# Six-layer decoder on one core: weights of the last three layers fetched and prepared inside the layer ahead, output stored batch by batch

## The chip, the cores and the metric

One core of one Trainium2 chip runs the whole program. The time is that of the device in microseconds (us), median of the runs. The engines are TensorE (PE), VectorE (DVE), ScalarE (ACT), GpSimd (POOL) and SyncE (SP, which only issues DMAs here); each runs its own instructions in order and waits for the others by semaphores.

## What is computed

Eight batches of x (256 x 512, float32) pass through six layers. After each, x becomes the layer norm of x plus the layer's output. In order:

```python
# attn0:  16 heads of 128, causal, rotary positions, one shared k/v head with gates
# xattn0: 32 heads of 16, keys and values from ctx_1024, axial rotary positions
# ffn0:   gated ffn of 1408, 8 experts of low rank on top of it, 2 chosen per token
# attn1:  16 heads of 32 over 4 kv groups, causal
# xattn1: 16 heads of 128 over 8 kv heads, keys and values from ctx_1024
# ffn1:   act_quant(rmsnorm(x)) @ ternary(w).T, hidden 2048, w3(silu(w1) * w2)
def _ternary_quant(w):
    s = jnp.mean(jnp.abs(w))
    wq = jnp.round(jnp.tanh(w / (s + EPS))) * jnp.arctanh(s)
```

A ternary weight is thus the sign of w where |w| is above a threshold that comes from the mean of |w| over the whole matrix, and zero elsewhere; the factor arctanh(s) is applied later (`c127`). All other weights and activations enter TensorE as a pair of float16 numbers, high and low part, and each product is three matmuls (high x high, high x low, low x high; `three`, L99).

## The kernel before

`build` (L2371) holds x in SBUF for the whole program and calls the six layers one after the other. Each layer is a `Scope`: it takes SBUF and semaphores, runs some blocks, and at its end POOL clears its semaphores in a block of its own (L70). A block ends when all engines have come to its end, so nothing of the next layer begins before. All loops over batches and heads are unrolled; within a layer's main block each engine has its own list, and the pipeline between them is written out by hand.

- **Weights.** Each of the first five layers begins with `load_and_split` (L106): SP issues 512 KB pieces (128 x 1024 float32) into a ring of 14 stages, ScalarE casts a piece to float16 (L137), VectorE subtracts the result from the piece and writes the low part (L143). TensorE and POOL have nothing to do in this block.
- **Counters.** In attn0, ffn0 and xattn1 the semaphores that count per batch start from one; a block of SP increments sets them (L90).
- **x.** In these three layers SP copies each batch of x within SBUF into `xcur` (L160), and TensorE transposes from there (L151); ScalarE and VectorE split the transposed x (L173, L180). A ninth, empty batch is copied and transposed at the end.
- **attn1** is `small_attention` (L707): steps t, one head each, with the projections, transposes and norms of neighbouring batches put into steps by a table (`at`). Per step ScalarE does the exponential and a cast, VectorE a maximum, POOL the low part of the probabilities.
- **xattn1** (L1604 and after): per batch 16 projections through four PSUM banks, then for i in 0 to 18: scores of head i, transposes of i-2, product with v of i-3, output projection of i-5. VectorE's list in one i is maximum, reciprocal of i-1, low part of the probabilities of i-2 and of the output of i-3; ScalarE's is the cast of i-2, the exponentials of i, the cast of i-3.
- **ffn1** (L1978) begins with `ternary_weights` (L1909): three 4 MB loads, Sign and Abs over 8192 columns per matrix on ScalarE, the sum of |w| on VectorE, one matmul that adds over partitions, then one compare-and-multiply per matrix (L1972). The gains g1, g2, g3 are fetched at the start of the main block (L2035), and POOL waits for them. The main block runs over 16 tiles of 128 rows, with four tiles in flight; iteration t of each engine's list works on tiles t to t-4.
- **Output.** After ffn1's scope has ended, one DMA of 4 MB stores all of x (L2432).

## Time and profile before

| what | us |
|---|---|
| median of 3 runs (lowest, highest) | 3574.78 (3571.34, 3575.84) |
| the profiled execution | 3574.41, its span 3572.6 |
| TensorE busy | 2898.9 (81%) |
| VectorE busy | 2107.8 (59%) |
| ScalarE busy | 1787.9 (50%) |
| POOL busy | 1404.3 (39%) |

Busy shares are means over stages with different limits, so they are read by stage. The page's forty slices (89 us each) show where TensorE dips, and where DMA is busy at the same time:

```profile
PE   3899989884888883899999778865999999952786
PEclk9988898996999996999999989987999999985998
DMA  4000000001000003000000000003000000030001
```

In a timeline row the columns are start, duration, engine, line, operation, tile written <- tiles read, shapes, count, and in brackets the idle time of the engine before it with the instruction that ended it. SPq rows are DMA issues.

### The profile page before, as it was taken

Reading aid. Unit: us, or ns where it says so; the run is one execution under the profiler, and the core shown is the slowest. Engines: PE = TensorE matmul, PEld = TensorE weight load, DVE = VectorE, ACT = ScalarE, POOL = GpSimd, SP = SyncE. Lnnn points to the kernel's source line nnn. Section 1 sums busy time; section 2 is a strip of 40 time slices with the busy share of each in tenths; the row PEclk is TensorE's granted clock in tenths of the full one; section 3 lists DMA queues with packets and bytes.
Section 4 is the critical chain, followed back from the end, with each engine's and each line's share of the span. In section 5 each row is a group of like instructions: output and inputs, shape, how many; then the busy total and the mean of one; then the engine's idle time right before and its main releaser. Section 6 shows DMA issues by size and latency. Waiting matters only on the chain. (4 is left out here: it accounts for less than half of the span.)

```text
span 3572.6 us, 64599 instructions
## 1 busy us (share of the span) xinstructions
PE 2898.9 (81%) x24890; PEld 2048.9 (57%) x24890; DVE 2107.8 (59%) x4526; ACT 1787.9 (50%) x3852; POOL 1404.3 (39%) x1539
## 2 busy tenths in 40 slices
PE   3899989884888883899999778865999999952786
PEld 2566655552566662777777666654666676631332
DVE  4666666665677775454455455655555555556886
ACT  3444444443788885233222256644444444445775
POOL 1333333332788883345444424440121112112553
PEclk9988898996999996999999989987999999985998
DMA  4000000001000003000000000003000000030001
GB/s 166 7 7 7 7 7 1 7 7 63 1 2 2 2 2 131 20 7 7 7 7 13 25 10 2 2 24 131 7 7 7 7 7 7 7 138 22 1 1 48
DMA packets 35031, 83.08 MB, mean 23 GB/s; under 512 B 5283, under 2 KB 9381, under 8 KB 33574
## 3 DMA queue, kind: packets, MB, share of 16 engines
q1 hardware_dynamic: 34726, 78.95, 5.9%
q8 instruction: 199, 3.26, 0.4%
q14 instruction: 106, 0.87, 0.1%
HBM read 60.59 MB, written 4.19 MB: 18 GB/s over the span
## 5 line engine op out<-in xcount | busy, mean ns | idle before, releaser
L873 POOL TENSOR_TENSOR c_pT<-c_prob,c_pT 128x512 f16<-128x512 f32 x256 | 293.3, 1159 | 106.5 <-ACT c_pT L832 105.8
L1686 POOL TENSOR_TENSOR c_prob<-c_prob,c_inv 128x512 f32<-128x512 f32 x128 | 133.2, 1041 | 244.1 <-DVE c_inv L1880 244.1
L1064 ACT ACTIVATE c_prob<-psT 128x512 f32<-128x512 f32 x256 | 155.9, 609 | 69.9 <-PE psT L995 56.0
L873 POOL TENSOR_TENSOR a_pT<-a_prob,a_pT 128x384 f16<-128x384 f32 x128 | 117.8, 924 | 183.6 <-ACT a_pT L832 183.5
L1143 DVE TENSOR_REDUCE c_peak<-psS 128x2 f32<-128x512 f32 x256 | 170.0, 684 | 20.6 <-PE psS L976 17.2
L832 ACT CAST c_pT<-c_prob 128x512 f16<-128x512 f32 x256 | 159.6, 624 | 0.0
L345 POOL TENSOR_TENSOR a_q_rot<-a_q_cos,a_q_sin 128x512 f32<-128x512 f32 x64 | 81.1, 1267 | 196.3 <-DVE a_q_sin L590 196.3
L1820 ACT CAST c_pT<-psT 128x512 f16<-128x512 f32 x128 | 75.1, 586 | 153.2 <-PE psT L1698 153.2
L353 POOL TENSOR_TENSOR a_prob<-a_prob,a_inv 128x128 f32<-128x128 f32 x128 | 51.3, 401 | 254.6 <-DVE a_inv L622 254.6
L520 ACT ACTIVATE a_pT<-psT,a_kvh_t 128x256 f16<-128x256 f32 (+1 forms) x256 | 93.8, 418 | 104.1 <-PE psT L366 104.1
L1390 POOL TENSOR_TENSOR f_ch<-f_h,f_c 128x256 f32<-128x256 f32 x88 | 76.3, 867 | 147.3 <-DVE f_h L1581 147.3
L101 PE MATMUL psP<-a_wq,a_xT 128*128 128x512 f16 x320 | 121.4, 379 | 13.6 <-DVE junk L594 10.4
L228 POOL TENSOR_TENSOR ln_rstd<-ln_ve,minus_half 128x1 f32<-128x1 f32 x48 | 32.0, 666 | 251.3 <-DVE ln_ve L213 251.3
L1812 ACT ACTIVATE c_prob<-psS,c_negmax 128x256 f32<-128x256 f32 x256 | 119.6, 477 | 21.7 <-DVE c_negmax L1873 20.7
L628 DVE SCALAR_TENSOR_TENSOR a_pT<-psT,a_kvh_t,a_pT 128x256 f16<-128x256 f32 (+1 forms) x256 | 95.0, 413 | 59.0 <-ACT a_pT L520 58.4
L1586 DVE TENSOR_TENSOR f_chs<-f_ch,f_chs 128x768 f16<-128x768 f32 x88 | 107.4, 1221 | 33.0 <-ACT f_chs L1526 32.3
L1873 DVE TENSOR_REDUCE c_negmax<-psS 128x2 f32<-128x512 f32 x128 | 88.3, 690 | 65.3 <-PE psS L1744 65.3
L976 PE MATMUL psS<-c_kS,c_qS 128*128 128x256 f16 x512 | 104.2, 288 | 25.4 <-DVE c_peak L1143 22.8
L103 PE MATMUL psP<-a_wq,a_xT 128*128 128x512 f16 x320 | 121.3, 379 | 0.0
L102 PE MATMUL psP<-a_wq,a_xT 128*128 128x512 f16 x320 | 121.3, 379 | 0.0
L2068 POOL TENSOR_TENSOR f_hg<-f_h,f_g 128x512 f32<-128x512 f32 x64 | 81.5, 1273 | 99.2 <-DVE f_h L2269 99.2
L1679 POOL COPY c_seen_now<-c_seen_col 128x2 f32<-128x2 f32 x9 | 1.7, 186 | 300.1 <-DVE c_qT L1866 253.0
(565 smaller groups left out, 11483.1 us busy)
## 6 DMA issues: line engine op xcount, KB each, us to landing
f_stage<-in_f_up_gateT SPq DMA_DIRECT2D x16, 352.0 KB, 7.9
c_stage<-in_L_xattn_Wq SPq DMA_DIRECT2D x10, 512.0 KB, 6.7
a_xcur<-x_all SPq DMA_DIRECT2D x9, 512.0 KB, 2.9
f_xcur<-x_all SPq DMA_DIRECT2D x9, 512.0 KB, 2.9
c_xcur<-x_all SPq DMA_DIRECT2D x9, 512.0 KB, 2.9
x_all<-in_x SPq DMA_DIRECT2D x1, 4096.0 KB, 13.9
a_stage<-in_L_attn_WqT SPq DMA_DIRECT2D x8, 512.0 KB, 7.5
a_stage<-in_L_attn_WoutT SPq DMA_DIRECT2D x8, 512.0 KB, 10.0
```

The source lines that it names most:

```text
L101: pe.matmul(out, a_hi, b_hi, start=first, stop=False, skip_group_check=True)
L102: pe.matmul(out, a_hi, b_lo, start=False, stop=False, skip_group_check=True)
L103: return pe.matmul(out, a_lo, b_hi, start=False, stop=last, skip_group_check=True)
L628: last = dve.scalar_tensor_tensor(pT[1][:, r, m, m * P:N], T[:, m * N + m * P:(m + 1) * N], kvh_t[:, m, H + h:H + h + 1], pT[0][:, r, m, m ...
L832: copy(pT[0][:, c % NPH, :], prob[:, c % NPX, :]).then_inc(p_high(c)[0], 1)
L873: pool.tensor_tensor(pT[1][:, c % NPH, :], prob[:, c % NPX, :], pT[0][:, c % NPH, :], ALU.subtract)\
L976: last = pe.matmul(S[:, first:first + w], qS[:, b % 2, h // HB, n * P:(n + 1) * P], kS[:, b % 2, k_of(h), 0:w], start=True, stop=not causa ...
L1064: act.activation(prob[:, c % NPX, :], ST[c % 2][:, 0:EW], ACT.Exp).then_inc(s.e_done, 1)
L1143: dve.tensor_reduce(peak[:, h, :], S, X_AXIS, ALU.max).then_inc(s.m_done, 1)
L1586: dve.tensor_tensor(chs[1][:, t % 2, :, :], ch[:, t % 2, :, :], chs[0][:, t % 2, :, :], ALU.subtract).then_inc(s.ch_lo.handle, 1)
L1686: pool.tensor_tensor(prob[:, h % NPB, :, :], prob[:, h % NPB, :, :], inv[:, h % NPB, :].rearrange("p (n a) -> p n a", a=1).broadcast_to([P ...
L1812: last = act.activation(prob[:, r, n, :], S[:, n * N:(n + 1) * N], ACT.Exp, bias=negmax[:, r, n:n + 1], accum_out=sums[:, r, n:n + 1])
```

## The change

1. Counters start from zero; the block that set them is gone. A wait for zero is left out (`after`). SBUF is laid out by hand (`place`, `plan`), so that weights of a later layer can be written while an earlier one runs.
2. TensorE transposes x straight from its place; the copies to `xcur` and the ninth batch are gone.
3. A class `Feed` fetches pieces of 512 KB into a ring of 3 or 4 stages (SP), and has calls for ScalarE and VectorE that handle one piece each, put into the lists by hand:
   - ffn0: 5 pieces (Wq, Wkv, Wo of attn1), one at the end of each of batches 1 to 5.
   - attn1: 16 pieces (Wk, Wv, context, Wq of xattn1), one every sixth step.
   - xattn1: 8 pieces of its own Wo in the projections of batch 0; 24 sums of |w| over 1024 columns of ffn1's matrices in batches 1 to 4 (every second head, on VectorE); the mean and threshold at the start of batch 7; 16 ternary pieces of w1 and w2 in batch 7, one per head. The gains are fetched in batch 7.
   - ffn1: 8 ternary pieces of w3 in iterations 1 to 3; the first output matmul waits for all of them.
4. Ternary pieces come in two kinds by turns: "sign" (Sign and Abs on ScalarE, one VectorE instruction) and "signs" (two VectorE instructions).
5. `load_and_split` is no longer called in attn1 and xattn1, and `ternary_weights` is gone.
6. The output is stored per batch from ffn1's main block.

```diff
+class Feed:
+    def fetch(self, sp, n):
+        for i in range(self.fetched, self.fetched + n):
+            if i >= self.ring:
+                sp.wait_ge(self.done, i - self.ring + 1)
+            sp.dma_start(self.staged(i), self.items[i][1]).then_inc(self.landed[i % self.ring], 16)
...
+    def high(self, act, n):
+        for i in range(self.high_at, self.high_at + n):
+            kind, src, hi, lo = self.items[i]
+            if kind == "split":
+                self.has_landed(act, i)
+                act.copy(hi, self.staged(i)).then_inc(self.high_done, 1)
+            elif kind == "sign":
+                self.has_landed(act, i)
+                act.activation(hi, self.staged(i), ACT.Sign).then_inc(self.signed, 1)
+                self.signs += 1
+                act.wait_ge(self.signed, self.signs)
+                act.activation(self.staged(i), self.staged(i), ACT.Abs).then_inc(self.high_done, 1)
...
+    def low(self, dve, n):
+        for i in range(self.low_at, self.low_at + n):
+            kind, src, hi, lo = self.items[i]
+            raw = self.staged(i)
+            if kind == "sum":
+                self.has_landed(dve, i)
+                last = dve.tensor_reduce(lo, raw.rearrange("p k (a n) -> p (k a) n", n=256), X_AXIS, ALU.add,
+                                         apply_absolute_value=True)
+            elif kind == "split":
+                dve.wait_ge(self.high_done, self.highs[i])
+                last = dve.tensor_tensor(lo, raw, hi, ALU.subtract)
+            elif kind == "sign":
+                dve.wait_ge(self.high_done, self.highs[i])
+                last = dve.scalar_tensor_tensor(hi, raw, self.thr[:, lo:lo + 1], hi, ALU.is_gt, ALU.mult)
+            else:
+                self.has_landed(dve, i)
+                m = self.mask[:, self.masks % 2, :].rearrange("p (k n) -> p k n", k=raw.shape[1])
+                dve.tensor_scalar(m, raw, self.thr[:, 3 + lo:4 + lo], None, ALU.is_lt).then_inc(self.masked, 1)
+                self.masks += 1
+                dve.wait_ge(self.masked, self.masks)
+                last = dve.scalar_tensor_tensor(hi, raw, self.thr[:, lo:lo + 1], m, ALU.is_gt, ALU.subtract)
+            last.then_inc(self.done, 1)
...
 # turn_x
-    pe.wait_ge(*s.xcur_ready.count(b, 16))
-            last = pe.transpose(banks[n][:, k * P:(k + 1) * P], xcur[:, n, k * P:(k + 1) * P], G.ident[:, :])
+                last = pe.transpose(banks[n][:, k * P:(k + 1) * P], G.x[:, b * NT + n, k * P:(k + 1) * P], G.ident[:, :])
...
 # small_attention: at the end of a step, ScalarE's and VectorE's list
+        def feeds(t):
+            return feed is not None and t >= 0 and t % 6 == 3 and t // 6 < len(feed.items)
+                    if feeds(t):
+                        feed.high(act, 1)
+                    if feeds(t):
+                        feed.low(dve, 1)
...
 # ffn0: behind the last hidden tile of a batch, ahead of the split of the next x
+                    if 1 <= b <= len(feed.items):
+                        feed.high(act, 1)
+                    if 1 <= b <= len(feed.items):
+                        feed.low(dve, 1)
                     x_low(dve, b + 1, s, xT, G.psS)
...
 # xattn1, ScalarE
+                        if b == 0 and i % 2:
+                            feed.high(act, 1)
+                    if b == B - 1:
+                        act.wait_ge(w_step, 5)
+                        act.activation(logs[:, 0, :], s_mean[:, :], ACT.Ln, bias=1.0)
+                        act.activation(logs[:, 1, :], s_mean[:, :], ACT.Ln, bias=1.0, scale=-1.0).then_inc(logs_done, 1)
...
                         if i >= 3:
                             hi_o(i - 3)
+                        if b == B - 1:
+                            feed.high(act, SIGNS[i])
...
 # xattn1, VectorE
+                        if b == 0 and i % 2:
+                            feed.low(dve, 1)
...
                         if i >= 3:
                             lo_o(i - 3)
+                        if 1 <= b <= 4 and 4 <= i < 16 and i % 2:
+                            feed.low(dve, 1)
+                        if b == B - 1:
+                            feed.low(dve, SIGNS[i])
...
 # ffn1
+                feed.fetch(sp, len(fed))
+                for b in range(B):
+                    sp.wait_ge(s.x_done, NT * (b + 1))
+                    sp.dma_start(G.out[:, b * NT:(b + 1) * NT, :], G.x[:, b * NT:(b + 1) * NT, :]).then_inc(out_done, 16)
...
+                    if 1 <= t <= 3:
+                        feed.high(act, (0, 3, 3, 2)[t])
...
+                    if 1 <= t <= 3:
+                        feed.low(dve, (0, 3, 3, 2)[t])
```

## Rows read from the trace of the kernel before

**Rows 1.** Busy time by stretch: length, PE, PEld, DVE, ACT, POOL, clock, DMA, GB/s

```profile
2404.20:2443.20 39.00, 0.00 (x0) 0.00 (x0) 29.35 (x24) 25.12 (x24) 0.00 (x0) 0.50 0.85 323
3183.80:3261.40 77.60, 0.59 (x2) 0.50 (x2) 53.28 (x14) 44.27 (x11) 0.16 (x3) 0.50 0.47 182
2910.00:3000.00 90.00, 84.90 (x635) 62.63 (x634) 46.31 (x94) 39.23 (x113) 18.17 (x19) 1.00 0.02 7
2210.00:2250.00 40.00, 33.46 (x437) 25.57 (x436) 23.65 (x59) 24.78 (x53) 18.48 (x21) 1.00 0.01 1
3387.00:3404.00 17.00, 13.79 (x74) 6.48 (x73) 14.65 (x31) 12.40 (x19) 9.01 (x8) 0.90 0.00 1
```

**Rows 2.** Timeline, start of ffn0's main block

```profile
1427.24 0.18 DVE L143 TENSOR_TENSOR f_wr<-f_stage,f_wr 128x32 f16<-128x32 f32 x1
...
1434.74 1.97 PE L156 MATMUL psS<-ident,f_xcur 128*128 128x128 f32 x8 [50.32 <-DMA f_xcur<-x_all]
```

**Rows 3.** Timeline, load ahead of attn1

```profile
2046.96 0.92 SPq L131 DMA_DIRECT2D a_stage<-in_L_attn_Wq  x2
...
2050.91 1.05 ACT L137 CAST a_wq<-a_stage 128x1024 f16<-128x1024 f32 x1 [17.20 <-DMA a_stage<-in_L_attn_Wq]
...
2058.97 0.35 SPq L843 DMA_DIRECT2D a_bias<-in_L_attn_bo  x1
```

**Rows 4.** Timeline, load ahead of xattn1 and start of its main block

```profile
2404.23 4.27 SPq L131 DMA_DIRECT2D c_stage<-in_L_xattn_Wq  x8
...
2412.44 1.22 DVE L143 TENSOR_TENSOR c_wq<-c_stage,c_wq 128x1024 f16<-128x1024 f32 x1 [0.59 <-ACT c_wq L137]
...
2443.19 0.24 SPq L1669 DMA_DIRECT2D c_seen_row<-in_seen  x1
```

**Rows 5.** Timeline, ternary block and start of ffn1's main block

```profile
3183.79 0.39 SPq L1931 DMA_DIRECT2D f_raw<-in_L_ffn_w1T  x1
...
3196.24 7.03 ACT L1943 ACTIVATE f_wq<-f_raw 128x8192 f16<-128x8192 f32 x1 [23.57 <-DMA f_raw<-in_L_ffn_w1T]
...
3227.07 26.08 DVE L1972 SCALAR_TENSOR_TENSOR f_wq<-f_raw,f_thr,f_wq 128x8192 f16<-128x8192 f32 x3
...
3240.13 1.28 ACT L1948 ACT_TABLE_LOAD   x1
...
3261.37 2.34 POOL L2052 TENSOR_TENSOR f_xg<-x_all,f_g 128x1024 f32<-128x1024 f32 x1 [7.55 <-DMA f_g<-in_L_ffn_g]
```

**Rows 6.** Timeline, end of ffn1 and the output

```profile
3556.25 0.55 DVE L2322 TENSOR_SCALAR x_all<-ln_r,ln_mv,ln_rstd 128x512 f32<-128x512 f32 x1 [0.66 <-POOL ln_rstd L2079]
3559.80 0.40 SPq L2432 DMA_DIRECT2D out_dram<-x_all  x1
```

**Rows 7.** Timeline, one head of xattn1 in batch 7, and the next maximum

```profile
3160.09 0.69 DVE L1873 TENSOR_REDUCE c_negmax<-psS 128x2 f32<-128x512 f32 x1 [0.59 <-PE psS L1744]
...
3161.01 0.48 ACT L1812 ACTIVATE c_prob<-psS,c_negmax 128x256 f32<-128x256 f32 x1
...
3161.92 0.38 ACT L1825 CAST c_qT<-psO 128x256 f16<-128x256 f32 x1
...
3162.33 0.42 DVE L1889 TENSOR_TENSOR c_qT<-psO,c_qT 128x256 f16<-128x256 f32 x1 [0.49 <-ACT c_qT L1825]
...
3163.35 0.69 DVE L1873 TENSOR_REDUCE c_negmax<-psS 128x2 f32<-128x512 f32 x1 [0.59 <-PE psS L1744]
```

**Rows 8.** Timeline, tables of xattn0: TENSOR_SCALAR from SBUF to SBUF

```profile
851.88 0.23 DVE L682 TENSOR_SCALAR c_ang<-c_ang 128x128 f32<-128x128 f32 x1
852.14 0.29 DVE L684 TENSOR_SCALAR c_turns<-c_ang 128x256 f32<-128x256 f32 x1
```

**Rows 9.** Timeline, ffn1, first gate of the iteration behind t = 1

```profile
3293.59 0.75 DVE L2269 SCALAR_TENSOR_TENSOR f_h<-psS,f_ax,f_sil 128x512 f32<-128x512 f32 x1 [0.81 <-ACT f_sil L2187]
```

**Rows 10.** Timeline, ffn1, the last step of a norm beside POOL's product

```profile
3405.13 2.19 DVE L2322 TENSOR_SCALAR x_all<-ln_r,ln_mv,ln_rstd 128x512 f32<-128x512 f32 x1
```

**Rows 11.** Timeline, ffn1, the last output matmuls

```profile
3548.38 5.28 PE L2137 MATMUL psO<-f_wq,f_hq 128*128 128x512 f16 x16 [2.58 <-DVE ln_ve L2316]
```

More of the change, by code:

```diff
@@ L79, in sb @@
     def sb(self, name, shape, dt):
-        return self.stack.enter_context(self.nc.sbuf_tensor(f"{self.tag}_{name}", shape, dt))
+        here, self.at = self.at, self.at + span(shape, dt)
+        assert self.at <= self.end, (self.tag, name, self.at)
+        return place(self.nc, f"{self.tag}_{name}", shape, dt, here)
     def counter(self, name, per_seq):
-        self.counters.append(Counter(self.sem(name), per_seq))
-        return self.counters[-1]
+        return Counter(self.sem(name), per_seq)
     def sem(self, name):
@@ L88, in sem @@
         return self.sems[-1]
-    def start_counters(self):
-        with self.nc.Block() as block:
-            @block.sync
-            def _(sp):
-                for counter in self.counters:
-                    sp.sem_inc(counter.handle, 1)
 def three(pe, out, a_hi, a_lo, b_hi, b_lo, first, last):
@@ L120, in load_and_split @@
     hi_done, lo_done = sc.sem("w_hi"), sc.sem("w_lo")
-    with nc.sbuf_tensor(f"{sc.tag}_stage", [P, NSTAGE, G.STAGE], F32) as stage, nc.Block() as block:
+    stage = place(nc, f"{sc.tag}_stage", [P, NSTAGE, G.STAGE], F32, sc.at)
+    with nc.Block() as block:
         def staged(i, p, k, n):
@@ L146, in kt_view, with split_pieces @@
+def split_pieces(src, hi, lo, k, n):
+    K, M = src.shape[1], src.shape[2]
+    out = []
+    for c in range(0, M, n):
+        for k0 in range(0, K, k):
+            at = (slice(None), slice(k0, k0 + k), slice(c, c + n))
+            out.append(("split", src[at], hi[at], lo[at]))
+    return out
 def kt_view(w):
     return w.rearrange("(k p) n -> p k n", p=P)
-def turn_x(pe, b, s, G, xcur, banks):
-    pe.wait_ge(*s.xcur_ready.count(b, 16))
-    for n in range(NT):
-        for k in range(KE):
-            last = pe.transpose(banks[n][:, k * P:(k + 1) * P], xcur[:, n, k * P:(k + 1) * P], G.ident[:, :])
-        last.then_inc(s.x_turned.handle, 1)
@@ L173, in x_high @@
 def x_high(act, b, s, xT, banks):
-    for n in range(NT):
-        act.wait_ge(*s.x_turned.count(b, n + 1))
+    for n in range(NT if b < B else 0):
+        after(act, s.x_turned, b, n + 1)
         act.copy(xT[0][:, :, n * P:(n + 1) * P], banks[n][:, :].rearrange("p (k t) -> p k t", k=KE))\
@@ L180, in x_low @@
 def x_low(dve, b, s, xT, banks):
-    for n in range(NT):
-        dve.wait_ge(*s.x_hi.count(b, n + 1))
+    for n in range(NT if b < B else 0):
+        after(dve, s.x_hi, b, n + 1)
         at = slice(n * P, (n + 1) * P)
@@ L1282, in ffn0 @@
     NU = 4
-    with Scope(nc, "f0") as sc:
+    with Scope(nc, "f0", G.low) as sc:
         def pair(name, shape):
@@ L1637, in xattn1 @@
         ones_b = sc.sb("ones_b", [P, P], BF16)
+        up = Scope(nc, "c1", G.a1_at)
+        prob = up.sb("prob", [P, NPB, NT, N], F32)
+        larger = sc.sb("larger", [P, 2, 1024], F16)
+        drams = [kt_view(W[f"L1_ffn_w{i}T"]) for i in (1, 2, 3)]
+        fed = split_pieces(kt_view(W["L1_xattn_Wo"]), wo[0], wo[1], 2, E)
+        for i, d in enumerate(drams):
+            for j in range(8):
+                k, c = divmod(j, 2) if i < 2 else (j, 0)
+                src = d[:, k:k + 1, c * 1024:(c + 1) * 1024] if i < 2 else d[:, 2 * j:2 * j + 2, :]
+                fed.append(("sum", src, None, part[:, i, 4 * j:4 * j + 4]))
+        for c in range(4):
+            for i in range(2):
+                for k in (0, 2):
+                    at = (slice(None), slice(k, k + 2), slice(c * E, (c + 1) * E))
+                    fed.append((("sign", "signs")[len(fed) % 2], drams[i][at], G.w12[i][at], i))
+        feed = Feed(sc, "feed", up.sb("feed", [P, 3, 1024], F32), fed, G.thr, larger)
+        NSUM = 24
+        SIGNS = [1] * H + [0] * 3
         NQ, NK, NV = H // 2, KVH // 2, NT * 2
@@ L1763, in project @@
                     def project(h):
-                        pe.wait_ge(*s.o_lo.count(b, h + 1))
+                        after(pe, s.o_lo, b, h + 1)
+                        if b == 0 and h % 2 == 0:
+                            pe.wait_ge(feed.done, h // 2 + 1)
                         for n in range(NT):
@@ L2133, in down @@
                             pe.wait_ge(s.var_ready, t)
+                        else:
+                            pe.wait_ge(feed.done, len(fed))
                         for k in range(KH):
```

530 lines of the change are left out of this document (273 added, 257 removed).

## The prediction

> **What bounds the kernel now.** I read four views, in this order: busy time and granted clock over chosen stretches, the timeline where one layer ends and the next begins, the timeline inside one steady step of each layer that is to take in new work, and the DMA issues. No engine is the bound of the whole span; each layer has its own, and between layers the kernel is serial. The reader is to see two stretches in which TensorE does nothing: before xattn1 it runs no matmul in 39.0 us while DMA is 85% busy and VectorE and ScalarE split weights, and ahead of ffn1 it is busy 0.6 of 77.6 us [rows 1]. Inside xattn1 it is the other way round: TensorE is busy 84.9 of 90 us at full clock, VectorE 46 and ScalarE 39. attn1 is milder (33.5 of 40 us, VectorE 24, ScalarE 25), and ffn1 is a chain over all engines (13.8, 14.7 and 12.4 of 17 us) [rows 1]. So the change takes work from places where everybody waits for it and puts it where somebody else is the bound. The question is how much of it shows there.
>
> **What goes.**
> 1. The copy of x ahead of the first transposes. In ffn0 VectorE is done with the weights at 1427.42 and TensorE begins at 1434.74 [rows 2]. In between lie the block that starts the counters and one DMA of x; both go. A plain block boundary takes about 0.3 us, so 7.0 us. attn0 begins in the same way: another 7.0. The later copies ran a batch ahead and cost nothing, so nothing more is gained by them. The transposes for a ninth batch go too, at the ends of three layers; I leave them out (0 to 2 us).
> 2. The load and split ahead of attn1: from the first issue at 2046.96 to the main block at 2058.97 is 12.0 us [rows 3].
> 3. The same ahead of xattn1: 2404.23 to 2443.19, 39.0 us [rows 4]. The mask set-up behind it stays.
> 4. The ternary block ahead of ffn1 and the gains' DMAs behind it: POOL's first product starts at 3261.37; after the change it can start where the first weight DMA is issued now, 3183.79, plus 0.3 [rows 5]: 77.3 us.
> 5. The output. Now the last x is ready at 3556.80, clearing the semaphores takes until 3559.80, and the 4 MB store ends with the span at 3572.6 [rows 6]. After it only the last batch's 512 KB is open at 3556.80. A 512 KB load takes 3.95 us from issue to the cast that waits for it [rows 3]; I take that, then the same 3.0 us of clearing: end at about 3563.9, 8.7 us less.
> Sum of 1 to 5: 14.0 + 12.0 + 39.0 + 77.3 + 8.7 = 151.0 us.
>
> **What comes in.** A split piece of 1024 columns is a cast of 1.05 us on ScalarE [rows 3] and a subtraction of 1.22 us on VectorE [rows 4], which waits for the cast.
> - ffn0, 5 pieces, one at the end of batches 1 to 5, ahead of the split of the next x. Nothing hides all of it, and all of it showing is 5 x 1.22 = 6.1 us. The cast falls where ScalarE waits for TensorE; I take 0.5 a piece: 2.5 us (0 to 6.1).
> - attn1, 16 pieces, every sixth step of about 2.5 us. There is room on average (ScalarE is idle 15 of 40 us), but VectorE stops at the piece until ScalarE, a little behind in its own program, has cast it. Behind that wait stand the next maximum and the splits that free TensorE's banks. All showing: 16 x 1.22 = 19.5 us; none: 0. I take a third, 7 us. In ScalarE's and SP's queues nothing is late: the pieces are 16 us apart, a load takes 4.
> - xattn1, batch 0, 8 pieces of Wo in the projections: per two projections VectorE has 2 x 0.69 + 1.22, TensorE about the same. 0.5 us (0 to 4).
> - xattn1, batches 1 to 4, 24 sums of 1024 columns on VectorE, every second head. One head takes 3.26 us, and VectorE idles 0.59 at its end waiting for TensorE [rows 7]. A sum is taken as long as a subtraction of that size, 1.22: 0.6 too long, but the loop described below needs only 2.5 of the 3.26, so the next head takes it up. Only the sum at each batch's end shows: 2 us (0 to 24 x 0.6 = 14).
> - Small steps: two short chains on VectorE at the ends of batches 5 and 7, the means in batch 7, and two logarithms with the table loads around them (1.28 us each [rows 5]) at a place where ScalarE waits for scores: 3 us (1 to 6).
> - **xattn1, batch 7: 16 ternary pieces, one per head.** This is the large term. Half are "sign": Sign and Abs on ScalarE, then a compare-and-multiply on VectorE. Half are "signs": a compare and a compare-and-subtract, both on VectorE. Follow one head [rows 7]: maximum at 3160.09, first exponential can start 0.72 later, the cast of o starts 0.91 behind it (3161.01 to 3161.92), VectorE's subtraction 0.41 behind that, and it is free 0.47 later. That is a loop of 2.51 us through two in-order engines, and TensorE's 3.26 hides it. A piece is put at the end of this loop on both engines. Prices: Sign and Abs did 8192 columns in 7.03 us [rows 5], so 1024 are as the cast, 1.05 each, with the wait between them 2.13; the compare-and-multiply is 26.08 us for 3 x 8192, 1.06 ns a column, as the split: 1.23. The short compare is not in the trace at this size; a TENSOR_SCALAR takes 0.23 us for 128 and 0.29 for 256 columns [rows 8], which carried on gives 0.65 to 0.7 (up to 1.22 if it runs like a subtraction). Sign head: 0.72 + 0.91 + 0.37 (the cast of o) + 2.13 + 1.28 = 5.4 us. Signs head: 2.51 + 0.07 + 0.7 + 1.25 = 4.5. Eight of each: 79.2 us against 16 x 3.26 = 52.2. Cost 27 us. Lower end: only VectorE's work counts. It is busy half of a batch [rows 1], so less than 2 us a head, and a piece is 1.6 on average: 3.6 a head at most, 5 us in all. Upper end: the compare at 1.22: 31 us, more if TensorE's clock falls (below).
> - **ffn1, 8 ternary pieces of w3** in iterations 1 to 3 (3, 3, 2), ahead of the next iteration's first gate. ScalarE can begin Sign about when that gate starts now (3293.59 [rows 9]). Iteration 1 (sign, signs, sign): Sign and Abs 2.1, then 1.25 + 1.95 + 1.25 on VectorE: 6.6 later. Iterations 2 (signs, sign, signs) and 3 (sign, signs): 2.1 + 1.25 + 1.95 = 5.3 each. Of 17.2 us the iteration takes back 1 to 1.5 each time, since VectorE then doesn't wait for silu (0.81 [rows 9]): 14 us (8 to 22).
> Sum: 2.5 + 7 + 0.5 + 2 + 3 + 27 + 14 = 56 us.
>
> The profiled execution is 3574.4 us long (span 3572.6), as good as the median of 3574.8. 3574.4 - 151 + 56 = 3479.4, less 1 for the ninth transposes: **3478 us**, 2.7% faster.
>
> The engines' common port is a place where the trace speaks against moving work. VectorE's TENSOR_SCALAR of 512 columns takes 2.19 us where it runs beside POOL's product of 1024 columns, and 0.55 at the end, where POOL has none left [rows 6, 10]. In xattn1 POOL's product ends before the piece starts; in ffn1's second iteration it does not. The Trainium skill, "GPSIMD Engine Reference", section "Specifications", says that POOL's SBUF interfaces are shared with VectorE and contend with VectorE instructions in a two-port mode or with two SBUF inputs. By that rule the splits in attn1 would be stretched too, as both their inputs lie in SBUF, and the sum would be some 5 us higher; by the trace's row alone, only the compares are.
>
> **The rivals.**
> - The loop is looser than I think (12%). Speaks for it: VectorE and ScalarE are half idle in xattn1 [rows 1]. Then batch 7 costs 5 us instead of 27: 3456.
> - TensorE's clock falls (15%). In batch 7 it works 3.1 us (94% of 3.26) out of about 5. After an idle of 2.58 us its next 16 matmuls of 512 columns take 5.28 us, where 16 x 512 columns at 2.4 GHz are 3.4 [rows 11], and ffn1 as a whole shows a granted clock of 0.90 where xattn1 has 1.00 [rows 1]. At 1.2 GHz a head's 3.1 us of TensorE are 6.2, 1.2 over my 5.0; over 16 heads that is 19 us, with 3 more in ffn1: 3500.
> - It does not do what it says in attn1 and ffn0 (10%): all 21 splits show because of VectorE's wait. 25.6 instead of 9.5: 3494.
> - ScalarE must load a table for Sign after Silu in ffn1 (5%). After Exp it did not (Sign at 3196.24 with none ahead) [rows 5]; after Silu no row shows it. Six loads of 1.28: 3486. The Trainium skill, "ScalarE: Activation LUTs", section "Table sets: the hidden batching unit", counts abs and identity among the functions in every set and does not list sign there; it leaves this open, and no row decides it.
> - Slower than before (2%): the clock stays at 1.2 GHz through whole batches of xattn1, because the gaps in VectorE's loop keep TensorE waiting. A batch has 84.9 us of matmuls in 90 [rows 1]; at half speed it takes some 170, 80 more. From 96 / 80 = 1.2 such batches on, the change loses; with batches 1 and 7 both slow the time would be 3638.
>
> **How the numbers follow.** 56% for the forecast, with its own range of 3462 to 3495. The range for all: downwards to just beyond the loose loop, 3450; upwards past the clock case to 3510, where also attn1's upper end and ffn1's lie. What is left out (both upper ends together with a fallen clock, or all terms at their lower ends) is under 2 in 10. About 0.2% (7 us) is what a measurement of this kernel can tell from no change. Faster by more than that: 0.97; within: 0.01; slower: 0.02.
>
> **What would show it.** In the profile after: TensorE's first matmul of ffn0 7 us nearer to the last split; no gap over 12 us between layers behind ffn0; attn1 no more than 8 us longer; batches 1 to 4 of xattn1 at 90 us each, batch 7 at 115 to 120, with VectorE's maxima 4.5 and 5.4 us apart in turn; granted clock there at 0.9 or above; first ffn1 iterations 4 to 6 us longer, with no ACT_TABLE_LOAD between Silu and Sign; end of the span 7 us after the last x. A batch 7 of 95 us, or maxima 3.5 us apart, would kill my loop; an attn1 longer by 15 us or more would kill the third that I took.

## The result and the profile after the change

The changed kernel takes 3480.69 us (median of 4 runs, 3479.75 to 3482.29) against 3574.49 us (3571.34 to 3575.84) beside it: a ratio of 0.9743, 95% interval 0.9729 to 0.9757. The prediction was 3478. The profiled execution took 3481.1 us, 93.3 less than that of before, with a span of 3479.1 us. So the total gives little away; the terms do. Each was measured from landmarks in the timelines: the first DMA of a stage's main block, and the rows in which VectorE writes a finished tile of x (two a batch; the first of the two unless the table says last).

| term | predicted | measured | from |
|---|---|---|---|
| attn0's start | -7.0 | -5.3 | first projection 54.65 -> 49.37 |
| ffn0's start | -7.0 | -6.9 | first finished x, after the shift ahead of the stage |
| load ahead of attn1 | -12.0 | -11.7 | last batch's first x in ffn0 to attn1's main block: 18.18 -> 6.45 |
| load ahead of xattn1 | -39.0 | -39.0 | the same, attn1 to xattn1: 43.42 -> 4.39 |
| ternary block, gains | -77.3 | -77.6 | last tile of x in xattn1 to POOL's first product: 81.63 -> 4.01 |
| output | -8.7 | -9.9 | last x to the end of the span: 16.35 -> 6.42 |
| ninth transposes | -1 | -1.0 | ffn0's last batch 74.75 -> 73.71 |
| ffn0, 5 splits | +2.5 | +1.4 | batches 74.75 -> 75.03 |
| attn1, 16 splits | +7 | +8.4 | main block to last x: 341.78 -> 350.22 |
| xattn1 batch 0, Wo | +0.5 | +1.6 | main block to first x: 99.72 -> 101.33 |
| 24 sums | +2 | +2.0 | batches 1 to 4: 90.84 -> 91.35 |
| batch 7, with small steps | +30 | +29.6 | 90.84 -> 120.42 |
| ffn1, 8 pieces of w3 | +14 | +15.0 | first product to last x: 294.88 -> 309.92 |
| sum | -96 | -93.4 | |

Busy time and granted clock of chosen stretches of the changed kernel (columns as in [rows 1]): a part of attn1, the heads of xattn1's last batch, and two stretches at the start of ffn1.

```profile
2210.00:2250.00 40.00, 31.85 (x423) 25.63 (x422) 25.54 (x61) 25.38 (x53) 17.31 (x20) 0.96 0.12 38
3070.00:3142.00 72.00, 47.41 (x308) 30.82 (x305) 47.56 (x77) 43.26 (x105) 14.97 (x14) 0.95 0.36 117
3160.00:3200.00 40.00, 16.72 (x64) 6.88 (x64) 17.46 (x28) 18.08 (x26) 13.17 (x11) 0.67 0.18 61
3200.00:3260.00 60.00, 38.31 (x182) 17.49 (x183) 47.26 (x88) 41.20 (x57) 27.08 (x23) 0.81 0.09 30
```

In the second row TensorE is busy 47 of 72 us, where it had 85 of 90 [rows 1]; its clock was granted at 0.95 all the same. In this batch no engine is busy all the time: they wait for each other in turn.

Timeline of the changed kernel at the starts of attn0, ffn0, xattn1 and ffn1 (start, duration, engine, line; in brackets the idle time ahead and what ended it):

```profile
44.45 1.94 PE L248 MATMUL psS<-ident,x_all 128*128 128x128 f32 x8 [44.45 <-PEq L136]
48.02 1.29 DVE L263 TENSOR_TENSOR a_xT<-psS,a_xT 128x512 f16<-128x512 f32 x2 [3.49 <-DMA a_rope_k<-in_rope_k]
49.37 0.39 PE L114 MATMUL psS<-a_wkv,a_xT 128*128 128x256 f16 x1 [2.97 <-DVE a_xT L263]
...
1421.85 0.19 DVE L157 TENSOR_TENSOR f_wr<-f_stage,f_wr 128x32 f16<-128x32 f32 x1
1422.36 1.94 PE L248 MATMUL psS<-ident,x_all 128*128 128x128 f32 x8 [43.35 <-PEq L136]
...
2385.56 0.55 DVE L1316 TENSOR_SCALAR x_all<-ln_r,ln_mv,ln_rstd 128x512 f32<-128x512 f32 x1 [0.44 <-POOL ln_rstd L983]
2388.97 0.26 SPq L1787 DMA_DIRECT2D c_seen_row<-in_seen  x1
...
3158.75 0.55 DVE L297 TENSOR_SCALAR x_all<-ln_r,ln_mv,ln_rstd 128x512 f32<-128x512 f32 x1 [0.44 <-POOL ln_rstd L306]
3162.76 2.34 POOL L2149 TENSOR_TENSOR f_xg<-x_all,f_g 128x1024 f32<-128x1024 f32 x1
```

In ffn0 TensorE begins 0.51 us behind the start of the last split instead of 7.50 [rows 2]: the full 7.0. In attn0 it begins 6.8 us sooner too, but the bracket in the second row tells where 1.7 of that went: VectorE waits for the DMA of the rope tables before it splits x. In the kernel before, that DMA was issued just ahead of the copy of x (at 46.76 and 47.32) and landed while TensorE waited for the copy. Ahead of xattn1 and ffn1 some 4 us stand where there were 43 and 82 [rows 4, 5].

Two heads of xattn1's last batch, VectorE and ScalarE, from one maximum over a sign piece and a signs piece to the third (the answer to [rows 7]):

```profile
3088.39 0.68 DVE L2030 TENSOR_REDUCE c_negmax<-psS 128x2 f32<-128x512 f32 x1
3090.27 1.07 ACT L196 ACTIVATE f_wq<-c_feed 128x1024 f16<-128x1024 f32 x1
3090.42 0.42 DVE L2046 TENSOR_TENSOR c_qT<-psO,c_qT 128x256 f16<-128x256 f32 x1 [0.69 <-ACT c_qT L1966]
3091.38 1.06 ACT L199 ACTIVATE c_feed<-c_feed 128x1024 f32<-128x1024 f32 x1
3092.47 1.28 DVE L215 SCALAR_TENSOR_TENSOR f_wq<-c_feed,thr,f_wq 128x1024 f16<-128x1024 f32 x1 [1.62 <-ACT c_feed L199]
3093.67 0.68 DVE L2030 TENSOR_REDUCE c_negmax<-psS 128x2 f32<-128x512 f32 x1
...
3096.04 0.74 DVE L219 TENSOR_SCALAR c_larger<-c_feed,thr 128x1024 f16<-128x1024 f32 x1
3096.82 1.28 DVE L222 SCALAR_TENSOR_TENSOR f_wq<-c_feed,thr,c_larger 128x1024 f16<-128x1024 f32 x1
3098.03 0.68 DVE L2030 TENSOR_REDUCE c_negmax<-psS 128x2 f32<-128x512 f32 x1
```

The maxima are 5.28 and 4.36 us apart (predicted 5.4 and 4.5), in turn from the fourth maximum to the end of the batch. VectorE no longer waits for TensorE ahead of a maximum; it waits 1.62 us for ScalarE's Abs, and the next head waits behind that.

The first w3 pieces of ffn1 on VectorE, and the gate behind them (it answers to [rows 9]):

```profile
3196.23 1.28 DVE L215 SCALAR_TENSOR_TENSOR f_wq<-f_feed,thr,f_wq 128x1024 f16<-128x1024 f32 x1 [3.19 <-ACT f_feed L199]
3197.43 0.75 DVE L219 TENSOR_SCALAR f_larger<-f_feed,thr 128x1024 f16<-128x1024 f32 x1
3198.21 1.28 DVE L222 SCALAR_TENSOR_TENSOR f_wq<-f_feed,thr,f_larger 128x1024 f16<-128x1024 f32 x1
3199.41 1.28 DVE L215 SCALAR_TENSOR_TENSOR f_wq<-f_feed,thr,f_wq 128x1024 f16<-128x1024 f32 x1
3200.61 0.75 DVE L2370 SCALAR_TENSOR_TENSOR f_h<-psS,f_ax,f_sil 128x512 f32<-128x512 f32 x1
```

Silu's table stays loaded: no ACT_TABLE_LOAD stands between Silu and Sign. From first gate to first gate the first four iterations take 21.7, 19.8, 19.8 and 17.8 us, where they took 15.9, 15.3, 15.6 and 16.4. In the second iteration one compare meets POOL's product of 1024 columns and takes 1.70 us instead of 0.75, as the prediction had read it from [rows 10].

The end, the last x and the last store (answers to [rows 6]); the span ends at 3479.1:

```profile
3472.68 0.55 DVE L2423 TENSOR_SCALAR x_all<-ln_r,ln_mv,ln_rstd 128x512 f32<-128x512 f32 x1 [0.66 <-POOL ln_rstd L2176]
3473.25 0.37 SPq L2136 DMA_DIRECT2D out_dram<-x_all  x1
```

### The profile page after: what moved, and what is told of

Read it like the earlier page. It is cut to its first block and busy times, and to the rows that moved or that the text cites. A ratio compares the mean times of both kernels' runs of the same rounds, so it can differ in the third digit from the quotient of the medians.

```text
span 3479.1 us, 64422 instructions
## 1 busy us (share of the span) xinstructions
PE 2910.5 (84%) x24866; PEld 2050.9 (59%) x24866; DVE 2108.0 (61%) x4574; ACT 1764.8 (51%) x3865; POOL 1404.9 (40%) x1537
## 3 DMA queue, kind: packets, MB, share of 16 engines
q8 instruction: 199, 3.26, 0.4%
## 5 line engine op out<-in xcount | busy, mean ns | idle before, releaser
L2211 PE MATMUL psS<-f_wq,f_xq 128*128 128x512 f16 x256 | 81.6, 477 | 56.1 <-DVE f_h L2370 49.7
L569 ACT CAST a_qT<-psT 128x512 f16<-128x512 f32 x64 | 36.7, 586 | 163.4 <-PE psT L442 163.4
```

Of the source, the lines that this page charges most:

```text
L2211: last = pe.matmul(U[2 * (j % 2) + i][:, :], xq[:, t % 2, i * KE + k, :], w12[i][:, k, c * E:(c + 1) * E], start=k == 0, stop=k == KE - 1)
```

## The experiments

All kernels start from the changed kernel. Stages that an edit doesn't touch are compared by their own lengths, because attn0 and xattn0 differ by some us from one execution to the next (last section).

**Loop or work in the last batch.** The first experiment only swaps an order:

```diff
                             hi_p(i - 2)
+                        if b == B - 1:
+                            feed.high(act, SIGNS[i])
                         if i < H:
                             expo(i)
                         if i >= 3:
                             hi_o(i - 3)
-                        if b == B - 1:
-                            feed.high(act, SIGNS[i])
```

> The changed kernel with one edit: in xattn1's last batch ScalarE does Sign and Abs of a piece ahead of the exponentials of that head, not at the end of the step. Same instructions, other order. Two theories on why a head takes 5.28 us (sign piece) or 4.36 us (signs piece) there. Loop theory (mine): VectorE's maximum, ScalarE's exponentials and cast, VectorE's subtraction and the piece follow each other, and VectorE waits 1.62 us for Abs; with the edit Sign and Abs fall where ScalarE waits 1.5 to 1.9 us for the maximum, so a sign head goes from 5.28 to about 4.0, a signs head stays at 4.36: 8 x 1.3 = 10 us less, about 3470. Work theory: what an engine has to do in a head sets its length, and the order doesn't matter: 3481, heads as before.

Measured: 3463.94 us, ratio 0.969 (0.9674 to 0.9706). The last batch went from 120.42 to 108.91 us, 11.5 less; the rest of the difference lies in attn0 and xattn0, where nothing was changed. A sign head takes 3.63 us, a signs head 4.36 as before. (One is 4.94.) The edited kernel's timeline, ScalarE and VectorE:

```profile
3079.16 1.06 ACT L196 ACTIVATE f_wq<-c_feed 128x1024 f16<-128x1024 f32 x1
3080.26 1.06 ACT L199 ACTIVATE c_feed<-c_feed 128x1024 f32<-128x1024 f32 x1
3080.42 0.68 DVE L2030 TENSOR_REDUCE c_negmax<-psS 128x2 f32<-128x512 f32 x1
3082.86 1.28 DVE L215 SCALAR_TENSOR_TENSOR f_wq<-c_feed,thr,f_wq 128x1024 f16<-128x1024 f32 x1
3084.05 0.69 DVE L2030 TENSOR_REDUCE c_negmax<-psS 128x2 f32<-128x512 f32 x1
```

Sign and Abs now run while ScalarE would wait for the maximum, and VectorE's piece has no wait ahead of it. The same instructions in another order are 1.65 us a sign head cheaper: the loop theory holds, the work theory doesn't.

The second takes ScalarE out:

```diff
-                    fed.append((("sign", "signs")[len(fed) % 2], drams[i][at], G.w12[i][at], i))
+                    fed.append(("signs", drams[i][at], G.w12[i][at], i))
```

> The changed kernel with all 16 pieces of the last batch of xattn1 made by VectorE alone (compare, then compare and subtract: 2.03 us of VectorE against 1.28 for a sign piece). Loop theory: every head takes the 4.36 us of a signs head, 8 x 0.92 = 7.4 us less, 3473. Work theory: VectorE, which has 3.9 us of work in a signs head, is the busiest engine of the pair of heads and gets 8 x 0.75 = 6 us more to do: 3487.

Measured: 3469.25 us, 0.9706 (0.9689 to 0.9722). From the fourth maximum on every head takes 4.35 or 4.36, and the batch 110.54, 9.9 less. VectorE, the busier of the two, had 6 us more to do, and the batch became shorter: what went was its wait for ScalarE. The work theory doesn't allow that. Batches 1 to 6 kept their lengths to 0.01 us in both runs.

**How far a head with extra work may lag.** Sums in six heads in a row (the second kernel has `1 <= b <= 2 and 4 <= i < 16` in the same place, twelve in a row):

```diff
-                        if 1 <= b <= 4 and 4 <= i < 16 and i % 2:
+                        if 1 <= b <= 4 and 7 <= i < 13:
                             feed.low(dve, 1)
```

> The changed kernel with the six sums of a batch (xattn1, batches 1 to 4) in six heads in a row, not in every second. Now the maxima are 3.71 and 2.81 us apart in turn and a batch is 0.51 us longer than before. Loop theory: a head with a sum needs 2.51 + 1.21 = 3.72 us, so six in a row push TensorE back by 6 x 0.46 less the first one that a buffer takes up: each batch 1.5 to 2.5 us longer, 3488. Work theory: VectorE has 1.9 + 1.2 = 3.1 us of work in such a head, under TensorE's 3.26: no change, 3481.

Measured: 3475.29 us, 0.9721 (0.9705 to 0.9738), and batches of 91.40 us against 91.35: no further cost, where I had expected 1.5 to 2.5 us each. Maxima of one batch, the last two with a sum ahead of them and the two behind:

```profile
2556.19 0.68 DVE L2030 TENSOR_REDUCE c_negmax<-psS 128x2 f32<-128x512 f32 x1
2559.69 0.68 DVE L2030 TENSOR_REDUCE c_negmax<-psS 128x2 f32<-128x512 f32 x1
2562.06 0.68 DVE L2030 TENSOR_REDUCE c_negmax<-psS 128x2 f32<-128x512 f32 x1
2565.12 0.69 DVE L2030 TENSOR_REDUCE c_negmax<-psS 128x2 f32<-128x512 f32 x1 [0.60 <-PE psS L1875]
```

Five of the six heads with a sum take 3.50 us, not my 3.72; the first takes 3.70, as a head with a sum does in the changed kernel (3.71, and 2.81 for the plain one behind it). Why a row of them is quicker isn't shown. Six of them lag by 1.65 us in all, and the next two heads, 2.37 and 3.06 apart, make up 1.1 of it. So the buffer is deeper than the one head that I had given it. Does it have an end?

> The changed kernel with the 24 sums in two batches of xattn1 (1 and 2), twelve heads in a row. The run with six in a row showed heads of 3.50 us, 1.65 us of lag at their end against TensorE's 3.26 a head, and no cost. Buffer theory: VectorE can lag TensorE by only some 1.5 to 2 us before TensorE waits; twelve in a row would lag 3.1, so these batches take 1 to 2 us more than the 91.4 with six, while batches 3 and 4 fall back to 90.84. Work theory: VectorE's 3.1 us of work stays under 3.26, no limit: 91.4.

Measured: 3478.93 us in one run. Batches 1 and 2 take 94.87 us, 3.5 more than with six sums; batches 3 and 4 are back at 90.83. From the fifth maximum to the last, all eleven intervals are 3.50 us: 38.5 against 34.8 in a plain batch, 3.7 more, and the batch is 4.04 longer than a plain one. Nothing is left to catch up in, so the whole lag shows. That there is a cost speaks against the work theory, but 3.5 us is more than the 1 to 2 of the buffer theory: a lag of a fixed 1.5 to 2 us isn't always forgiven. What the two runs fit is that the heads behind make up what they can before the batch ends.

**attn1: wait or work.**

```diff
-                    if feeds(t):
+                    if feeds(t - 1):
                         feed.low(dve, 1)
```

> The changed kernel with VectorE's subtraction of a piece in attn1 one step later than ScalarE's cast. attn1 is 8.4 us longer than before the change; VectorE waits for the cast in 10 of 16 places, 14.0 us in all, and the subtractions are 19.6 us of work. If VectorE's wait is what shows (my prediction's reason), the cost falls to 2 to 4 us and the time to about 3476. If it is the work itself (19.6 us more of VectorE and 17 of ScalarE in a stage where TensorE is busy 0.83), the stage keeps its length: 3481.

Measured: 3474.48 us, 0.9715 (0.9698 to 0.9731); attn1 takes 347.19 us, 3.0 less than after the change, 5.4 more than before it. So the wait isn't all of the cost (2 to 4 us would have been left), and the work isn't either (nothing would have changed). Where this stage was untouched, it took 350.2 to 351.4 us in eight profiled executions; with this edit 347.16 to 347.19 in three. VectorE's waits for the cast fell from 14.0 to 2.7 us. But the 16 subtractions, 19.6 us before this edit (1.21 to 1.23 each), now take 23.0 us. Two of them with the POOL product that they meet:

```profile
2112.23 1.22 DVE L212 TENSOR_TENSOR c_wv<-a_feed,c_wv 128x1024 f16<-128x1024 f32 x1
2112.29 1.92 POOL L960 TENSOR_TENSOR a_pT<-a_prob,a_pT 128x384 f16<-128x384 f32 x1 [3.16 <-ACT a_pT L917]
...
2137.11 0.91 POOL L960 TENSOR_TENSOR a_pT<-a_prob,a_pT 128x384 f16<-128x384 f32 x1 [1.63 <-ACT a_pT L917]
2137.17 1.93 DVE L212 TENSOR_TENSOR c_cT<-a_feed,c_cT 128x1024 f16<-128x1024 f32 x1
```

The first of the two takes its usual time, 1.22 or 0.91 us. The second takes its own time plus nearly all that the first has left: 0.71 of 0.85 us in the lower pair, 1.0 of 1.16 in the upper; other pairs of this run also come out 0.13 to 0.15 short of the whole. The two don't share, they queue. The Trainium skill, "SBUF — State Buffer", section "SBUF: two separate sides", says so: the port pair of VectorE and GpSimd is an exclusive lock, held by whoever starts first for the whole instruction, when VectorE's operation has two SBUF inputs. The trace agrees with that but for these 0.14 us.

In the changed kernel none of the 16 subtractions was stretched. The ten that waited began within 0.02 us of the end of POOL's product: the cast of `a_pT` that releases the product stands directly ahead of the piece's cast in ScalarE's list, and both end together. At the other six no product was under way. But POOL's products met subtractions there too, two of them less than 0.1 us behind the start of one:

```profile
2175.51 1.22 DVE L212 TENSOR_TENSOR c_cT<-a_feed,c_cT 128x1024 f16<-128x1024 f32 x1
2175.58 1.92 POOL L960 TENSOR_TENSOR a_pT<-a_prob,a_pT 128x384 f16<-128x384 f32 x1 [0.32 <-ACT a_pT L917]
```

What are the other 5.4 us? Two kernels, each without one half of the work:

```diff
-                last = dve.tensor_tensor(lo, raw, hi, ALU.subtract)
+                if self.tag == "a1":
+                    last = dve.memset(raw[:, 0:1, 0:1], 0.0)
+                else:
+                    last = dve.tensor_tensor(lo, raw, hi, ALU.subtract)
```

```diff
-            if kind == "split":
+            if kind == "split" and self.tag == "a1":
+                pass
+            elif kind == "split":
...
-                dve.wait_ge(self.high_done, self.highs[i])
+                if self.tag == "a1":
+                    self.has_landed(dve, i)
+                else:
+                    dve.wait_ge(self.high_done, self.highs[i])
```

> The changed kernel without VectorE's 16 subtractions in attn1 (a one-element memset stands in for each; the low halves of xattn1's weights are zeros, set ahead of the stage, so the output is not the reference's); ScalarE's casts stay. What is read is the length of attn1's main block: 341.8 us before the change, 350.2 after, 347.2 with the subtraction one step later. What do the remaining 5.4 us consist of? Theory A: VectorE's work, stretched where it runs beside POOL; then casts alone cost at most 2 us: 342 to 344. Theory B: ScalarE's casts hold up the exponentials and the banks that ScalarE frees; then casts alone already cost 4 us or more: 346 and up.

> The counterpart: without ScalarE's 16 casts in attn1 (the high halves are zeros, set ahead of the stage, so the output is not the reference's); VectorE's subtractions stay and wait for the piece's DMA alone. Theory A (VectorE's work): 345 to 347 us of main block. Theory B (ScalarE's casts): 342 to 344.

Measured, one run each (3476.82 and 3486.91 us): main block 344.86 us without the subtractions, 351.44 without the casts. The first kernel isn't quite "casts alone": its memset still waits for the cast, 9.4 us in six places. So casts and waits together cost 3.1 us; subtractions without casts or waits cost 9.7, where the changed kernel with all three costs 8.4 (8.4 to 9.6 in the eight executions), and the one with the subtraction a step later 5.4. VectorE's subtractions are the larger part (theory A), but neither theory gives these numbers, and the terms don't add up: taking casts and waits away from the changed kernel saved nothing that can be seen. In the kernel without casts the subtractions take 22.4 us instead of 19.6, since seven of them begin while POOL's product runs; how much of the 9.7 that makes isn't shown. Which of VectorE's steps the subtraction delays where it stands, these runs don't tell; that stays open.

**ffn1: the pieces in the waits of the first iterations.**

```diff
-        fed = [(("sign", "signs")[j % 2], w3_dram[:, 2 * j:2 * j + 2, :], w3[:, 2 * j:2 * j + 2, :], 2) for j in range(8)]
+        fed = [("signs", w3_dram[:, 2 * j:2 * j + 2, :], w3[:, 2 * j:2 * j + 2, :], 2) for j in range(8)]
...
+                    if t <= 3:
+                        feed.low(dve, 1)
                     move_x(t)
+                    if t == 0:
+                        feed.low(dve, 2)
                     gate(t - 1, 3)
...
-                    if 1 <= t <= 3:
-                        feed.low(dve, (0, 3, 3, 2)[t])
+                    if t in (1, 2):
+                        feed.low(dve, 1)
```

> The changed kernel with the eight w3 pieces of ffn1 all made by VectorE alone and put where it waits while the first iterations fill the pipeline: one ahead of each of the first four moves of x, two behind the first, one at the end of iterations 1 and 2. Before this edit these eight cost 15.0 us. Gap theory (mine): VectorE's work costs only where no wait takes it; it waits 3.9, 4.2, 2.1, 1.7 and 1.5 us at the places chosen, a piece is 2.03 us, and at most 4 us of the 15 stay: about 3470. Work theory: 8 x 2.03 = 16 us of VectorE in a chain over all engines show wherever they stand: 3481.

Measured: 3464.47 us, 0.9705 (0.969 to 0.9719). From the last x of xattn1 to the last of ffn1 it is 303.40 us instead of 313.93: 10.5 of the 15.0 are gone and 4.5 are left. The first piece, with the move of x behind it:

```profile
3163.28 0.75 DVE L219 TENSOR_SCALAR f_larger<-f_feed,thr 128x1024 f16<-128x1024 f32 x1
3164.06 1.28 DVE L222 SCALAR_TENSOR_TENSOR f_wq<-f_feed,thr,f_larger 128x1024 f16<-128x1024 f32 x1
3167.22 0.69 DVE L2358 TENSOR_SCALAR f_xq<-psT 128x1024 f16<-128x1024 f16 x1 [1.87 <-PE psT L2198]
```

VectorE still waits 1.87 us behind it, so the piece cost nothing. The gap theory holds, if not to the number (at most 4 us were to stay, 4.5 did). VectorE's pieces are 18.2 us of work here and 14.2 in the changed kernel, and the stage is 10 us shorter.

**The last batch: use the projections.**

```diff
-    G.w12 = [f1.sb(f"wq{i}", [P, KE, 2048], F16) for i in range(2)]
+    w2 = f1.sb("wq1", [P, KE, 2048], F16)
+    f1.at = G.c1_at + 2 * span([P, KE, 2048], F16)
+    G.w12 = [f1.sb("wq0", [P, KE, 2048], F16), w2]
...
-        SIGNS = [1] * H + [0] * 3
+        SIGNS = [0, 1] * 8 + [0] * 3
...
+                        if b == B - 1 and i >= NK + NV:
+                            feed.low(dve, 1)
```

> The changed kernel with all 16 pieces of xattn1's last batch made by VectorE alone; the eight of w1 go into the place of wk and wv, which are free sooner, and are made in the query projections, one each, and the eight of w2 in every second head. Now this batch costs 29.6 us more than a plain one, and 19.7 with one VectorE piece in every head. Loop theory, with the buffer that the run with six sums in a row showed: a head with a piece takes 4.36, the next 2.4 to 2.8, the pair 6.8 to 7.2 against 6.52, so the heads cost 1 to 5 us; a projection has 0.69 + 2.03 = 2.7 us of VectorE against 2.6 of TensorE, 1 to 3 us in all; small steps 2: the batch at 95 to 101 us, the time about 3457. Work theory: the same 16 pieces, the same 19.7 us: 3471.

Measured: 3457.26 us, 0.9682 (0.9668 to 0.9697); the batch takes 96.83 us, 6.0 more than a plain one. Of these 6.0, 0.8 lie ahead of the first maximum, and from the first maximum to the last it is 47.35 us against 42.42. Most of that, 3.6 us, falls on the first four intervals, which are quick in a plain batch (7.65 us in all); from the fifth maximum on the heads are 2.37 and 4.37 apart in turn, 6.74 a pair against 6.52. In the projections VectorE works without a pause, one projection every 2.62 us:

```profile
3060.13 0.69 DVE L2017 SCALAR_TENSOR_TENSOR c_qT<-psO,c_qT 128x512 f16<-128x512 f32 x1
3060.74 0.74 DVE L219 TENSOR_SCALAR c_larger<-c_feed,thr 128x1024 f16<-128x1024 f32 x1
3061.52 1.28 DVE L222 SCALAR_TENSOR_TENSOR f_wq<-c_feed,thr,c_larger 128x1024 f16<-128x1024 f32 x1
3062.75 0.69 DVE L2017 SCALAR_TENSOR_TENSOR c_qT<-psO,c_qT 128x512 f16<-128x512 f32 x1
```

The same 16 pieces cost 19.7 us with one in every head and 6.0 here. The place decides.

**The output in one store again.**

```diff
-                for b in range(B):
-                    sp.wait_ge(s.x_done, NT * (b + 1))
-                    sp.dma_start(G.out[:, b * NT:(b + 1) * NT, :], G.x[:, b * NT:(b + 1) * NT, :]).then_inc(out_done, 16)
+                sp.wait_ge(s.x_done, NT * B)
+                sp.dma_start(G.out[:, :, :], G.x[:, :, :]).then_inc(out_done, 16)
```

> The changed kernel with one part undone: the output in one store of 4 MB behind the last x, no longer batch by batch. The last x is ready at 3472.7 and the span ends 5.9 us behind it (its end was 15.8 us behind it before). If the store alone made that difference: span end 15 to 16 us behind the last x, the time 9 to 10 us longer, 3490. Rival: most of it was the clearing of the semaphores, which now runs at another place; then 4 us or less.

Measured: 3486.21 us (3482.42 to 3489.14), 0.9758 (0.9744 to 0.9773). The last x starts at 3471.25 and the span ends at 3487.4, 16.15 us later against 6.42: 9.7 us more, with nothing else changed, out of 9.9 gained. So the single large store makes nearly all of the difference, and the place of the clearing next to none. The medians differ by 5.5 us only, within what attn0 and xattn0 do from one execution to the next.

**All together.** One kernel with the later subtraction in attn1, the two edits of xattn1's last batch and of ffn1, and in attn0

```diff
                 dve.memset(g_cum[:, 0:1], 0.0)
-                dve.wait_ge(consts, 32)
                 x_low(dve, 0, s, xT, G.psS)
+                dve.wait_ge(consts, 32)
```

> All edits that the theories call good in one kernel: VectorE's subtractions in attn1 one step later, w1 in the query projections and w2 in every second head of xattn1's last batch, w3's pieces in the waits of ffn1's first iterations, and in attn0 VectorE splits the first x before it waits for the rope tables' DMAs. That last wait took the place of the x copy: TensorE's first matmul came 6.8 us sooner, the first projection only 5.3. Expected of it: first projection at 47.6 instead of 49.4. If the savings add up: 3481 - 3 (attn1) - 23 (last batch) - 11 (ffn1) - 1.7 = 3442. If a later stage gives one back (ffn1's first iterations against a colder TensorE, say), 3450 or more.

Measured: 3439.2 us (3436.83 to 3440.46), 0.9631 (0.9618 to 0.9644). Stage by stage: first projection at 47.74 instead of 49.37 (main block at 44.34 and 44.40); attn1 347.16; the last batch 98.27; ffn1 304.90. These are 1.6, 3.1, 22.2 and 9.0 us less, 36 in all, and xattn0, which nobody touched, was 5 us shorter in this execution. The savings nearly add up. What is missing lies in the last batch, 1.4 us more than alone, and in ffn1, 1.5. The second can't be told from chance: where ffn1 was untouched, it took 312.5 to 314.7 us from xattn1's last x, and the next kernel, with the same ffn1, took 303.7. The first comes with the clock, in this kernel's timeline and stretch:

```profile
3071.16 0.66 PE L1825 MATMUL psT<-ident,c_prob 128*128 128x128 f32 x4 [2.60 <-POOL c_prob L1813]
3072.69 0.63 PE L115 MATMUL psP<-c_wo,c_qT 128*128 128x512 f16 x1
...
3070.00:3076.00 6.00, 4.84 (x23) 2.84 (x24) 4.67 (x8) 3.00 (x11) 2.08 (x2) 0.72 0.26 87
```

TensorE had stood still for 2.60 us; then its matmuls of 512 columns took 0.63 us instead of 0.38 and the granted clock of these 6 us is 0.72, partly at 1.2 GHz. The kernel with the last batch's edit alone has the same idle at the same place, and there the clock stayed at 2.4 GHz:

```profile
3083.75 0.66 PE L1825 MATMUL psT<-ident,c_prob 128*128 128x128 f32 x4 [2.60 <-POOL c_prob L1813]
3085.11 0.38 PE L115 MATMUL psP<-c_wo,c_qT 128*128 128x512 f16 x1
...
3082.58:3088.58 6.00, 4.83 (x35) 3.59 (x36) 4.67 (x9) 3.59 (x12) 2.08 (x2) 1.00 0.27 87
```

So the idle alone doesn't bring the fall; what decides it, these runs don't show. It is the rival that I gave 15%, at a fifteenth of its price.

Last, the sums moved into the query projections of batches 1 to 3 as well:

```diff
-                        if 1 <= b <= 4 and 4 <= i < 16 and i % 2:
-                            feed.low(dve, 1)
...
-                        if b == B - 1 and i >= NK + NV:
+                        if (b == B - 1 or 1 <= b <= 3) and i >= NK + NV:
                             feed.low(dve, 1)
```

> The kernel with all good edits (3439) and one more: the 24 sums of xattn1 stand in the query projections of batches 1 to 3, eight each, not in the heads of batches 1 to 4. A query projection gives 2.6 us to VectorE, which has 0.69 of work there; a sum is 1.21. Room theory: batches 1 to 4 fall from 91.35 to 90.84, 2.0 us less, 3437. Rival: a sum holds up the split that frees a bank, and each of the 24 shows with some tenths: 3440 to 3445.

Measured: 3438.44 us (3432.03 to 3442.27), 0.9628 (0.9615 to 0.9641). Batches 1 to 4 take 90.83 us each, as before any change, and xattn1's main block is 2.1 us shorter than in the kernel above. The total can't tell the two apart; the trace can. This is the fastest of all, 1.2% below the changed kernel by the medians.

## Why the prediction was right, and where it wasn't

**The gains** came out at 151.4 us against 152. Five of the seven are within 0.3 us, since each was a serial stretch that could be read off between two rows. Two were off, in opposite ways. In attn0 the step "so 7.0 us ... another 7.0" failed: I priced the start by its likeness to ffn0 and didn't ask what is late next. The DMA of the rope tables was, 1.7 us, and moving one wait behind the splits gave 1.6 back. The output gained 1.2 more than I took: the last 512 KB and the clearing took 5.9 us behind the last x, not 7 (and my own terms end at 3563.8, not 3563.9).

**The last batch** was right in mechanism: heads of 4.36 and 5.28 us against 4.5 and 5.4, and the two swaps show why. That its total came to 29.6 against 30 is partly luck. Of the 29.6, 29.1 lie between the first maximum and the last (71.48 us against 42.42), where I had put 27; 0.5 lie behind, and nothing ahead. I had taken every plain head as 3.26 us, but the first four intervals of a plain batch take only 7.65 us together, so the heads cost more than I said. The 3 us for small steps made up for it: the logarithms with their table loads end at 3071.42, 0.4 us behind the end of the first maximum, and don't show otherwise. With 29.6 us the loose loop (3456) falls. What I had not seen is how little of the price was needed: 11.5 of the 29.6 us went with the order of ScalarE's list alone.

**The sums** had the right price, 2.0, for the right reason: a head with a sum takes 3.71 us, the next 2.81, a pair 6.52 as without sums, and only the last one of a batch shows. That a single head is all that can make up a lag, as I then took it, doesn't hold: behind six sums in a row two heads did, behind twelve none was left.

**attn1** cost 8.4 against 7, within its bounds, and past the 8 that I had named as the most. "I take a third" was a guess, and that it came near is luck. I had named VectorE's wait for the cast as the cause. Casts and waits together cost 3.1 us; the subtractions cost 9.7 without either, and 5.4 together with casts that stand one step ahead. I also read the port wrongly. The sentence that by the row alone only the compares would be stretched is refuted: subtractions that meet POOL's product take up to 1.94 us. The rule that I quoted from the Trainium skill, "GPSIMD Engine Reference", was right. In the changed kernel's attn1 it shows on POOL's side alone (1.92 us instead of 0.91), because no subtraction there began during a product.

**ffn1** cost 15.0 against 14, with no table load. The first iterations were longer by 5.8, 4.5, 4.2 and 1.3 us; I had said 4 to 6 for three. The sum of what was given back was about right, as far as a stage that differs by up to 2 us between executions can tell.

**ffn0 and batch 0** were 1.4 against 2.5 and 1.6 against 0.5: the errors cancel. Why batch 0 costs 1.6 wasn't taken apart.

**The clock** hardly took part: 0.95 over the heads of the last batch, and 0.87 over ffn1 from its first product to its last x, against 0.88 before. The rival that all 21 splits show (25.6 us) falls too: 9.8 us. So does the slower one: no batch came near 170 us.

## What to carry to other kernels

Work moved off a serial stretch must be priced where it lands, by the loop that it lengthens: follow one step through all in-order queues, and put the piece where its own engine would wait, not at the end of the step. The same 16 pieces cost 29.6, 19.7 or 6.0 us by place and kind, small steps included, and a stretch in which a pipeline fills, or a phase bound by another engine, took them at a fraction of that price. When a wait is removed, look for the next thing that the same instruction waits for.

## What the runs showed of the hardware

- VectorE's and POOL's operations with two SBUF inputs queue behind each other: 1.93 us instead of 1.22 on one side, 1.92 instead of 0.91 on the other, each 0.14 us less than its own time and the rest of the other's. A wait ahead of such an operation can cost less than it seems: without 11.3 us of waits, 16 subtractions took 3.4 us longer.
- xattn1's plain batches repeat to 0.02 us over all runs, at a granted clock of 1.00. attn0 and xattn0 do not repeat so well: where they were unchanged, attn0's main block took 772.0 to 775.0 us and xattn0's 525.4 to 531.1 in the profiled executions. The granted clock over 510 us of xattn0 was 0.92 in a short one and 0.91 in a long one. In totals, an effect under about 5 us needs the stage's own length.
- An idle of 2.60 us in a stage at full clock was followed by matmuls of 512 columns at 0.63 us in two kernels, and cost 1.4 us there; in a third the same idle at the same place was followed by 0.38 us at full clock and cost nothing.
